# Second cross attention: the scores of both head halves as one block of products with one signal, and another order of the last steps before the experts

## The reference, cut to what matters

```python
def _L1_xattn_ref(x, cls, w_kv, w_q, w_la, w_proj, b_proj, att_weight):   # 16 heads of 8
    k, v, q = ...                                   # projections of x (context) and cls (rows)
    attn = softmax(q @ k.T * SCALE)
    gate = 0.5 * mean(x @ w_la) + 0.5 * max(x @ w_la)         # one number for each head
    attn2 = softmax(gate * attn)
    out = (w * attn2 + (1.0 - w) * attn) @ v
    return out @ w_proj + b_proj

def _L1_ffn_ref(x, ...):                            # on the normalised rows of the result
    scores = softmax(xt @ gate_w.T)
    idx = top_k(scores + gate_bias, 2)
    for e in range(8):
        h = silu(xt @ w1[e].T) * (xt @ w3[e].T)
        y = y + gate_e * (h @ w2[e].T)
    z = silu(xt @ sw1.T) * (xt @ sw3.T) @ sw2.T     # two shared experts
    return y + z
```

## Time and profile before

| what | value |
|---|---|
| median of three runs | 4233.28 us |
| the profiled execution | 4226.67 us, of which the profile's span is 4224.8 us |
| busy in the span | PE 96%, DVE 83%, ACT 71%, POOL 68% |
| second cross attention, first to last score block of half 0 | 3630.43 to 3968.29 us |
| from there to the first downward product of the experts | 3968.29 to 4008.56 us |

### The profile page before, as it was taken

How to read it: one execution, slowest core, us unless ns; L and a number is a source line. 1 busy time by engine, 2 the same in 40 slices (tenths; PEclk the granted TensorE clock), 3 DMA queues, 4 the chain that set the end, 5 groups by cost and what they waited for, 6 DMA issues and landing times.

```text
span 4224.8 us, 147350 instructions
## 1 busy us (share of the span) xinstructions
PE 4047.6 (96%) x50345; PEld 2794.5 (66%) x50345; DVE 3507.6 (83%) x7187; ACT 3012.7 (71%) x6848; POOL 2884.0 (68%) x3647
## 2 busy tenths in 40 slices
PE   5999998999999999999999999999999999899899
PEld 3777775666666666666666666666666666566565
DVE  4666667999889998899998999899999999577776
ACT  3555556888888888788887888788888888455422
POOL 2333337888878888788887888888888988465400
PEclk9999999999999999999999999999999999887899
DMA  3000001000000001000010001000010000000000
GB/s 90 8 6 7 6 4 48 10 8 9 24 21 9 8 9 33 14 7 10 13 32 9 9 9 29 18 7 10 7 36 10 10 7 8 18 13 11 6 10 10
DMA packets 162234, 64.89 MB, mean 15 GB/s; under 512 B 121557, under 2 KB 156129, under 8 KB 162017
## 3 DMA queue, kind: packets, MB, share of 16 engines
q1 hardware_dynamic: 162016, 62.05, 5.8%
HBM read 26.54 MB, written 2.10 MB: 7 GB/s over the span
## 4 chain that ended last, share of the span: by engine, by line
POOL 42%; PE 27%; issue 22%; DVE 5%; POOLq 2%; SPq 1%; ACT 1%; DVEq 0%; DMA 0%; ACTq 0%
POOL qn L650 11%; POOL qn L639 8%; POOL big L650 7%; POOL e L645 6%; POOL big L639 4%; PE pj L1623 3%; PE pp L1581 2%; PE sc L1883 2%; PE po L1596 2%; PE po L1907 2%; PE sc L1993 2%; PE pj L1615 2%; PE pj L1664 1%; POOL rstd L661 1%; PE po L1602 1%
## 5 line engine op out<-in xcount | busy, mean ns | idle before, releaser
L1690 PE MATMUL pj<-wqkv,xcT 128*128 128x512 f32 x1536 | 800.8, 603 | 17.8 <-issue 9.5
L650 POOL TENSOR_TENSOR qn<-qn,big 128x512 f32<-128x512 f32 x384 | 491.3, 1280 | 294.9 <-DVE big L1209 294.9
L862 ACT ACTIVATE big<-pj 128x512 f32<-128x512 f32 x768 | 474.0, 617 | 69.4 <-PE pj L1690 58.5
L1209 DVE TENSOR_TENSOR big<-pj,ropes 128x512 f32<-128x512 f32 x768 | 522.1, 680 | 0.0
L1215 DVE TENSOR_REDUCE ss<-big 128x8 f32<-128x512 f32 x768 | 515.5, 672 | 0.1
L650 POOL TENSOR_TENSOR big<-big 128x512 f32<-128x512 f32 x384 | 485.9, 1276 | 4.6 <-DVE big L1209 4.6
L1843 PEld LDWEIGHTS pp<-wo,oT 128*128 128x128 f32 x3072 | 357.3, 191 | 161.2 <-ACT oT L885 81.0
L645 POOL TENSOR_TENSOR e<-e,rc 128x512 f32<-128x512 f32 x384 | 401.0, 1044 | 54.4 <-DVE rc L1239 54.4
L639 POOL TENSOR_TENSOR qn<-qn,ny 128x512 f32<-128x512 f32 x384 | 397.3, 1045 | 7.5
L639 POOL TENSOR_TENSOR big<-big,ny 128x512 f32<-128x512 f32 x384 | 396.9, 1045 | 7.6
L1697 PE MATMUL pj<-wqkv,xcT 128*64 128x512 f32 x1536 | 394.8, 614 | 0.8 <-DVE big L1209 0.7
(11 more groups left out here) (320 smaller groups left out, 9976.5 us busy)
## 6 DMA issues: line engine op xcount, KB each, us to landing
wqkv<-in_L_ffn_Wqkv SPq DMA_DIRECT2D x18, 512.0 KB, 3.8
xsd<-Y SPq DMA_DIRECT2D x192, 32.0 KB
xsd<-Y SPq DMA_DIRECT2D x384, 15.8 KB
xsf<-Y SPq DMA_DIRECT2D x96, 64.0 KB
xsf<-Y SPq DMA_DIRECT2D x192, 31.5 KB
xsx<-Y SPq DMA_DIRECT2D x64, 64.0 KB, 1.8
xsx<-CT SPq DMA_DIRECT2D x64, 64.0 KB, 1.9
wo<-in_L_ffn_Wo SPq DMA_DIRECT2D x6, 512.0 KB, 4.4
```

Source lines behind the costliest of these rows:

```text
L650: nc.gpsimd.tensor_tensor(U[a.par][i], U[a.par][i], t2b[i % 2], ALU.add).then_inc(sem("d_add"), 1)
L862: nc.scalar.activation(sqb[i % 2], pj[i % 2][:, :], ACT.Square).then_inc(sem("d_sq"), 1)
L1209: nc.vector.tensor_tensor(t2v, swapped, sin, ALU.mult).then_inc(sem("d_r"), 1)
L1690: mm(pj[i % 2][:, :], xcT[:, a.par, :], wqkv[:, i * 512:i * 512 + 512], start=True, stop=True).then_inc(sem("d_ch"), 1)
```

## The change

It does these things. (1) TensorE issues the scores of a tile as one block, both halves one after the other, at the place where half 0 stood, and signals once; it waits for both subtractions of the tile before. The block of half 1 at the head of the step is gone. The counts that others wait for on `l_s` follow. (2) In the last steps of the stream VectorE normalises a tile ahead of its routing operations and not at the head of the next step, and the routing of the 28 tiles is cut at other places. (3) TensorE issues the upward products of experts 0 and 1 ahead of the last two row tiles' transposes. (4) ScalarE takes the Silu of experts 0 and 1 ahead of the last four tiles' exponential; VectorE does the first two routing operations of these tiles inside the experts' first group, and the others of them are spread anew.

```diff
@@ -716,7 +716,7 @@
                             past(pool, "l_kq", tile.g + 1)
-                            past(pool, "l_s", tile.g * 2 - 2)
+                            past(pool, "l_s", tile.g - 1)
                         kk = l_kq[i][:, 0, :].rearrange("p (b t) -> p b t", b=BT)
@@ -972,7 +972,7 @@
                         past(act, "l_pj", tile.g + 1)
-                        past(act, "l_s", tile.g * 2 - 2)
+                        past(act, "l_s", tile.g - 1)
                         nc.scalar.copy(l_kq[tile.par % 2].rearrange("p a t -> p (a t)"), pj[0][:, 0:2 * P]).then_inc(sem("l_kq"), 1)
@@ -1055,15 +1055,18 @@
             nc.scalar.copy(CT[:, NT - 2:NT, :].rearrange("p a t -> p (a t)"), r_rows).then_inc(sem("r_c"), 2)
-            act.wait_ge(sem("r_st"), ROUTE_STEPS + 2)
-            nc.scalar.activation(r_buf[0][:, FIRST:NT, :], r_buf[0][:, FIRST:NT, :], ACT.Exp).then_inc(sem("r_e"), 1)
-
-            with act.Fori(0, NM) as m:
+            def m_group(m, known):
                 for ex in range(NEX):
+                    if known and ex == 2:
+                        act.wait_ge(sem("r_st"), ROUTE_STEPS + 2)
+                        nc.scalar.activation(r_buf[0][:, FIRST:NT, :], r_buf[0][:, FIRST:NT, :], ACT.Exp).then_inc(sem("r_e"), 1)
                     act.wait_ge(sem("m_h"), m * NEX + (ex + 1))
-
                     act.wait_ge(sem("m_hT"), m * NEX + max(ex - 1, 0))
                     nc.scalar.activation(e[:, ex % 2, :], h_banks[ex % 2][0][:, :], ACT.Silu).then_inc(sem("m_silu"), 1)
+
+            m_group(0, True)
+            with act.Fori(0, NM - 1) as i:
+                m_group(i + 1, False)
 
@@ -1334,7 +1337,7 @@
                     if tile:
-                        past(dve, "l_s", tile.g * 2 + (h + 1))
+                        past(dve, "l_s", tile.g + 1)
                         nc.vector.tensor_reduce(h8(mx, 0, h), by_head(sc[:, h * 512:h * 512 + 512]), AX, ALU.max).then_inc(sem("l_mx1"), 1)
@@ -1412,7 +1415,9 @@
 
-                normalise(p[6])
+                ending = p[3] is None and p[6] is not None
+                if not ending:
+                    normalise(p[6])
                 inverse1(p[3])
@@ -1430,12 +1435,16 @@
                 aggregate(p[4])
-                for stage, (first, n) in ROUTED.items():
-                    if p[stage] and isinstance(p[stage].g, int) and p[stage].g == NT - 1:
-                        route(first, n)
+                if p[3] and isinstance(p[3].g, int) and p[3].g == NT - 1:
+                    normalise(p[5])
+                    route(0, 7)
+                if ending and p[4]:
+                    normalise(p[5])
+                    route(7, 10)
+                    normalise(p[4])
+                    route(10, ROUTE_STEPS)
 
             tt, reduce, stt = nc.vector.tensor_tensor, nc.vector.tensor_reduce, nc.vector.scalar_tensor_tensor
-            ROUTED = {3: (0, 7), 4: (7, 15), 5: (15, ROUTE_STEPS)}
 
@@ -1501,8 +1510,6 @@
             stream(dve, NT, l_step, 0, 0, 7, 4)
-            route_rest(0, 2)
-
             acc = oT[:, 0:MT, :]
@@ -1515,7 +1522,7 @@
                     if known:
-                        route_rest(2 + 2 * ex, 4 + 2 * ex)
+                        route_rest(2 * ex + (ex > 2), 2 * ex + 2 + (ex > 1))
                     dve.wait_ge(sem("m_y"), m * NEX + (ex + 1))
@@ -1871,16 +1878,16 @@
 
-                def scores(tile, h):
-                    if tile:
-                        if h == 0:
-                            past(pe, "l_km", tile.g * 2 + 2)
-                        past(pe, "l_sb1", tile.g * 2 - 1 + h)
+                def scores(tile):
+                    if tile:
+                        past(pe, "l_km", tile.g * 2 + 2)
+                        past(pe, "l_sb1", tile.g * 2)
                         past_waits(pe, "went_on")
-                        r = slice(h * 64, h * 64 + 64)
-                        for bb in range(BT):
-                            q = slice(bb * 64, bb * 64 + 64)
-                            last = mm(sc[q, h * 512:h * 512 + 512], l_kq[tile.par % 2][r, 1, q], l_km[tile.par % 2][r, bb], start=True, stop=True)
+                        for h in range(2):
+                            r = slice(h * 64, h * 64 + 64)
+                            for bb in range(BT):
+                                q = slice(bb * 64, bb * 64 + 64)
+                                last = mm(sc[q, h * 512:h * 512 + 512], l_kq[tile.par % 2][r, 1, q], l_km[tile.par % 2][r, bb], start=True, stop=True)
                         last.then_inc(sem("l_s"), 1)
@@ -1946,7 +1953,6 @@
 
-                scores(p[2], 1)
                 values2(p[4], p[6])
@@ -1955,7 +1961,7 @@
                 values1(p[2], p[6])
-                scores(p[1], 0)
+                scores(p[1])
                 turn2(p[3], 1)
@@ -1997,6 +2003,7 @@
             up(0, True, 0)
+            up(0, True, 1)
             past(pe, "l_y", NT)
@@ -2014,7 +2021,7 @@
                 for ex in range(NEX):
-                    if ex + 1 < NEX:
+                    if ex + 1 < NEX and (ex or not known):
                         up(m, known, ex + 1)
```

## The result

The kernel after runs in 4180.36 us (median of four runs, 4178.48 to 4181.39), beside 4232.33 us for the kernel before (4227.32 to 4238.9). The ratio is 0.9876, with a 95% interval of 0.9859 to 0.9893: 52 us faster. Forecast were 4177 us. The profiled execution took 4181.39 us, 1.9 us of it outside its span.

What follows compares the result with a forecast made beforehand. TensorE, 97 to 99% busy at an unsteady clock, was taken to bind, its replies almost as tightly at 2.4 GHz. Terms -4.7, -47, -1.3 and -3 gave -56: 4170.7 us, 4177 as median; range 4160 (-68) to 4212.

Steps and rivals of the forecast that it cites:

- The block: Merged scores on TensorE: four quarters run together in 1.1 us, saving 1.0 us a step at 2.4 GHz, 1.9 at 1.2.
- The step: Second cross attention at 2.4 GHz: VectorE's chain ends last and comes 0.44 us earlier, 9.05 us a step instead of 9.49.
- The price of the clock: 24 steps before: 42.5 us lost to 95.6 us at 1.2 GHz, 0.444 us for each.
- The falls: Drops of TensorE's clock to 1.2 GHz in the 24 steps: once or twice, at most three, instead of nine; some 4 us each.
- my mechanism: Clock falls after a step's thin end; a block filling four quarters, twice as dense, and a 5% shorter step help it hold.
- 24 steps: Stretch 3670.38 to 3940.63: 217.2 us instead of 270.25, -53, with 1.5 falls left -47.
- The end: Last products through experts' start: -3 us, from 0 to -5; normalising ahead of routing starts VectorE's reciprocal 2.6 us earlier.
- The table loads: Two more on ScalarE around the moved Exp, 2 x 1.28 us, covered by the third upward pair; uncovered they cost 2.6 us.
- (b): Rival: half of the falls stay, four to six; about -38 us, 4195 us; chance 0.18.
- (a): Rival: clock falls as often as now, mean step 10.56 us; -23 us with opening and end, 4210 us; chance 0.15.
- (c): Rival: late replies idle TensorE some 0.5 us a step and 1.2 GHz spreads; 4244 us and more; chance 0.04.
- (d): Rival: the merged block's quarters run in turn, step 9.98 us, +15 us, 4248 us; chance 0.02.

Runs made afterwards that it cites:

- the doubled projection: Changed kernel with each output projection issued twice: 4176.55 us, ratio 0.9856; the same edit in the kernel before: 4215.14 us, ratio 0.9947.
- the repetition: The changed kernel itself measured again, nothing altered, on the chip of the last group of runs: 4183.78 us, ratio 0.9874.
- the longer chain: Changed kernel with two extra small VectorE products (16 columns, unused tile) behind the first maximum: 4184.31 us, ratio 0.9874.
- the end alone: Kernel before with only the new order of the end (parts 2 to 4), scores still in two blocks: 4228.77 us, ratio 0.9985.
- the reordered kernel: Changed kernel with first products ahead of the second softmax's transposes on TensorE, and ScalarE's order to match: 4231.65 us, ratio 0.9981.

## Why the prediction was right

The forecast was 4177 us, the median is 4180.36. The way there, step by step.

*The block.* Right. 1.09 us for four products of half-size tiles in two banks. Line 1567 was the right row to trust: here a second pair of quarters adds 0.01 us to the first. The Trainium skill ("TensorE: Matmul & The Clock Gate", Measured speedup vs the span model) gives 3.07 times for four row strips; the 1.4 us that I had estimated from it didn't come.

*The step.* 9.05 forecast, 9.06 measured. The chain came out at every link within 0.04 us. What I had wrong is where TensorE would wait: not 0.2 us ahead of the first transposes but 0.55 us ahead of the router row, for ScalarE's copy of the group just before. The removed block had stood between these two and hidden the copy. It doesn't set the step: VectorE's chain ends later, and TensorE had room for another 0.22 us (the doubled projection, step 9.06).

*The price of the clock.* 42.5 us for 95.6 us was too much. Each first step of a pass of the loop of four takes longer, in both kernels. TensorE after, the score blocks and what it waits for in such a step:

```profile
3703.13 1.09 PE L1890 MATMUL sc<-big,kbuf 64*64 64x512 f32 x8
...
3712.18 1.09 PE L1890 MATMUL sc<-big,kbuf 64*64 64x512 f32 x8
...
3714.91 0.30 PE L1942 MATMUL po<-K,xsd 128*128 128x128 f32 x1 [0.83 <-ACT big L1010]
...
3720.28 0.38 PE L1969 MATMUL po<-egT,tmp 128*128 128x8 f32 x2 [0.39 <-issue]
...
3721.95 1.09 PE L1890 MATMUL sc<-big,kbuf 64*64 64x512 f32 x8
```

9.05 us, then 9.77, with the clock at 2.4 GHz throughout. The wait for ScalarE's copy is 0.83 us in place of 0.55, and 0.39 us more stand before the router product, with no releaser in the profile. The six such steps took 9.77 to 9.86 us, the first of them 10.27: 5.0 us over six plain ones. Before they were 10.0 against 9.49, 3.1 us in all, which I had booked as clock; what is left, 39.4 us, is 0.41 for each of the 95.6. What lies behind the loop's head was not examined.

*The falls.* One or two were forecast, up to three; there were five, and my mechanism can't say how many. They were worth less than the 4 us each: four of them lasted 3.4 us and made their steps 1.1 to 1.3 us longer, the fifth lasted 10.2 and cost 3.4 (a step of 12.44 us), 8.2 us together. They lay where the nine had lain: four began inside a score block, one 0.2 us ahead of one. So the term "24 steps" was mis-sized: -53 + 6 = -47 forecast, -39.6 measured, which is 217.4 for the steps, 5.0 for the loop's heads and 8.2 for the clock. Of the 7.4 us between them the heads, which the forecast of 24 x 9.05 put at nothing, are 5.0 and the clock 2.2. In the repetition the steps took 224.6 us, -45.6. The forecast stood on where the falls had lain, and the experiments bear out the direction (denser work there, faster kernel), not a rule.

*The end.* -3 forecast, -5.4 measured. The normalising is worth more than I gave it; of the Silu's place no gain is shown. A part of the 5.4 us is the clock's: 20.5 us of the stretch ran at 1.2 GHz, 27.3 before. With the whole end and 27.3 us at 1.2 GHz (the profile of the longer chain) the stretch is 37.07 us, 3.2 under the kernel before, which is nearly my -3. In the end alone it ran 35.2 us at 1.2 GHz, and the gain in that profile was 0.6 us. I had kept back up to 4.4 us for a later return of the clock; it came earlier instead: over the five profiles with the merged block and the whole end 20.5 us of this stretch were at 1.2 GHz three times, 17.1 and 27.3 once each.

*The table loads.* Hidden, as said. No load showed a drain: 3962.95 + 1.28 is 3964.23, and the Exp starts at 3964.24. The Trainium skill ("ScalarE: Activation LUTs", What ACT_TABLE_LOAD costs) adds a drain of some 1.38 us to a load; this trace doesn't show it.

*The rivals.* (b), half of the falls, is what the first profile shows by count (five), but not by price: 24 us at 1.2 GHz in place of 95.6, and the time came out as forecast. (a), as many falls as before, and (c), slower through the clock, didn't come; the reordered kernel shows something like (c): more waits, a clock of 0.84 and the gain lost. (d), quarters in turn, is refuted by the 1.09 us.

*Slips in the working.* The sums of (a) and (c) leave out the end's -3; with it (a) is 4207. A sum of -68 gives 4165 and not 4160 on the scale of the median. The stretch up to 3680.60 has TensorE busy for 96%, not 97. None of them changes the verdict.

That the sum hit within 4 us is in part luck: the terms missed by +7 and -2. On the profiles' own scale the forecast was 4170.7 us and the execution took 4181.39, 10.7 more, of which 5.6 lie in code that is the same. Between the medians less of it shows, since the profiled execution before was faster than its four timed runs and the one after the slowest of its four.

## What to carry to other kernels

Small products in different row halves and column halves of the array belong next to each other in the queue: the second pair is free. When TensorE is nearly full and its clock is not at 1.00, ask first where the thin work lies: a doubled product there, in time that TensorE had to spare, made a kernel faster by 20 us. And what leaves a queue may have hidden a neighbour's reply: look for the wait that takes its place, and judge the clock from many timed runs, not from one profile.

## What was not expected of the hardware

VectorE's last subtraction in a step takes 0.69 us alone. In the changed kernel it overlaps GpSimd's masked key rows, and the timelines read, VectorE and GpSimd after, then both before:

```profile
3777.58 1.40 DVE L1381 TENSOR_TENSOR qn<-qn,mx 128x512 f32<-128x512 f32 x1
```

```profile
3776.39 2.05 POOL L721 TENSOR_TENSOR big<-kbuf,K 128x512 f32<-128x512 f32 x2 [0.67 <-ACT kbuf L976]
```

```profile
3791.23 0.68 DVE L1378 TENSOR_TENSOR qn<-qn,mx 128x512 f32<-128x512 f32 x1
```

```profile
3790.26 2.56 POOL L721 TENSOR_TENSOR big<-kbuf,K 128x512 f32<-128x512 f32 x2 [0.89 <-ACT kbuf L976]
```

After, GpSimd's two instructions end at 3778.44 in 2.05 us, and VectorE's subtraction lasts 1.40, ending 0.54 later; before, VectorE's takes 0.68 and GpSimd's pair 2.56. One of the two is held up each time, by 0.5 to 0.7 us, as if they took turns. The trace agrees here with the Trainium skill ("SBUF — State Buffer", SBUF: two separate sides), which has a VectorE operation with two inputs in SBUF and a GpSimd operation that reads SBUF share a pair of ports that one of them holds for its whole instruction; both are so here, and the one that started first wasn't held up. It costs nothing here, since VectorE waits for the next score block anyway (0.25 us at 3771.63); with VectorE at 87% of the stretch it may be what a next change meets first.
